# An RWKV layer with its decay totals moved to their own buffer and its hand-written order of steps rewritten on four engines

## The chip, the core and the metric

The kernel runs on one core of one Trainium2 chip, in one launch. The metric is the device time of that launch in microseconds: the median of the runs. All data are float32. Five kinds of engine work at once, each through its own list of instructions in the order in which they are written: TensorE (PE in the rows), VectorE (DVE), ScalarE (ACT), GpSimd (POOL) and SyncE (SP), whose queue starts the DMAs. They meet only at semaphores, so where an instruction waits, everything behind it on its engine waits too.

## What is computed

One RWKV layer over 8 batches of 256 tokens with 512 channels (32 heads of 16). Cut to what matters:

```python
xn  = ln(x) ;  sx = token_shift(xn)
xxx = tanh((xn + sx*maa_x) @ maa_w1) ; xxx = xxx @ maa_w2          # five small mixes
x5  = xn + sx*(maa_stack + xxx)                                    # five mixed inputs
w   = exp(-exp(time_decay + tanh(x5[1] @ decay_w1) @ decay_w2))
r, k, v, g = x5[3] @ Wr.T, x5[0] @ Wk.T, x5[2] @ Wv.T, silu(x5[4] @ Wg.T)
def step(s, rkvw):
    a = k[:, None] * v[None, :]
    return a + w[:, None]*s, r @ (u*a + s)                         # 256 steps in time, state 16x16 a head
att = groupnorm(scan(step)) * gn_w + gn_b
x   = x + (att*g) @ Wo.T
xn2 = ln(x) ; sx2 = token_shift(xn2)
kk  = relu((xn2 + sx2*ffn_maa_k) @ ffn_Wk.T)**2
x   = x + sigmoid((xn2 + sx2*ffn_maa_r) @ ffn_Wr.T) * (kk @ ffn_Wv.T)
```

## The kernel before, in words

A batch passes through four parts, and each part is cut into named steps. `n_` steps are the statistics and the norm of the raw input. `f_` steps (front) make the five mixed inputs and the projections k, v, r: `f_xin`, `f_lora0/1`, `f_m20` to `f_m24` (small matmuls of the mixes; `f_pair1`, `f_pair3` in the first batch), `f_mix0` to `f_mix4`, `f_dec1/2` (the decay), `f_k0` to `f_k3`, `f_v..`, `f_r..`. `b_` steps (back) are g (`b_g0` to `b_g3`), the recurrence inside blocks (`b_prod` on GpSimd, `b_score` on TensorE, `b_mul` and `b_red` on VectorE, `b_add` on GpSimd), the doubling of the decays over blocks of 1, 2, 4 and 8 tokens (`b_step1/2/4/8` on VectorE), the chunk states (`b_vtok`, `b_ktok`, `b_kv0/1`, `b_scan`, `b_exp`, `b_acc`, `b_apply0` to `3`), group norm, the output projection `b_wo` and the second layer norm. `c_` steps (tail) are the feed-forward part: `c_fk`, `c_fr0/1`, `c_fv0/1`, `c_mul`, `c_out`.

The work is pipelined over batches. `walk` (line 302) makes each engine's list: one round holds the tail of batch b-2, the back of batch b-1, the front of batch b and the norm of batch b+1. The rounds in order are `first` (front of batch 0), `second` (front of 1, back of 0), five times `main` (four of them in a hardware loop of two passes), `end`, `last`, and the feed-forward tail of batch 7. Which step follows which in a round is written out by hand for each engine and kind of round in the dictionary `ORDER` (lines 50 to 124).

The dictionary is the same for issue on every engine, but what a step waits for stands in the step. Those that matter here:

- `f_centre` (VectorE, lines 1436 to 1448) takes the head means out of the value weights. It waits for the DMA that loads `wv` (line 351, the first of the large loads).
- `f_xin` (lines 1185 to 1208) makes the input of the small mixes, channel tile by channel tile. In the first batch it waits for ScalarE's normed input. `f_lora1` on TensorE (line 605) waits for each tile of it.
- `b_step1` (line 1263) multiplies the decays into k and r once `b_prod0` has read them. The products of decays ("totals", lines 265 to 268 and 1258 to 1261) are kept in the tile `ktok`, which also holds the second norm's output (`cen`, `xhat2`). Line 1270 waits, before the first total is written, until TensorE has transposed that output.
- `b_norm2` on VectorE (line 1524) waits for ScalarE's copies of those same transposes.
- `b_exp` (line 1392, and line 1065 on ScalarE) spreads the scanned states over heads for `b_apply0` to `3` on TensorE, which take them in the order VectorE, ScalarE, VectorE, ScalarE. `f_mix1` to `4` run on GpSimd at about the same time.
- SyncE: `stage(b)` loads the raw input of batch b once four scores of batch b-2 are done. `turn(b)` swaps two halves of a small tile, `thB` to `thR`, once `f_lora0/1` of batch b are through their tanh.

## Time and profile before

| | us |
|---|---|
| median of 3 runs | 771.14 |
| lowest and highest run | 769.87, 771.64 |
| span of the profiled execution (first to last instruction) | 768.0 |
| first round (0 to 52.4) | 52.4 |
| second round (52.4 to 137.9) | 85.5 |
| five main rounds and the end round, by the start of `c_fk` | 90.4, 90.3, 88.2, 87.0, 88.3, 87.3 |
| last round and feed-forward tail | 98.5 |

The profile lists the span of the profiled execution and not its time as the runs measure it; the median lies 3.1 us above the span, for what is around the instructions. Rounds are told apart by the first instruction of `c_fk` (line 856), at 137.92, 228.27, 318.59, 406.82, 493.80, 582.12 and 669.46 us.

In a row of the timeline, the first number is the start in us from the span's start, the second the time from start to end, `xN` the number of instructions merged, and the bracket the idle time of the engine before them with what ended it. "issue" there is a wait for nothing that the profile shows.

### The profile page before, as it was taken

The numbers are of one execution on the slowest core, as the hardware profiler recorded it, in microseconds if no ns is written. First come the engines' busy times: TensorE is split into PE (matmuls) and PEld (weight loads), VectorE is DVE, ScalarE is ACT, GpSimd is POOL, SyncE is SP. The second block draws the span as 40 slices with busy tenths as digits, with TensorE's granted clock in tenths as the row PEclk, the third lists the DMA queues.
The fourth block names the chain that finished last, engine by engine and source line by source line (L and its number), as shares of the span: only waits on it lengthen the run. The fifth ranks groups of instructions, "written<-read, shape, count | busy, mean of one in ns | idle before, by whom it ended". The sixth has DMA issues, their size and how long they took to land.

```text
span 768.0 us, 17247 instructions
## 1 busy us (share of the span) xinstructions
PE 691.9 (90%) x7260; PEld 480.3 (63%) x7260; DVE 509.0 (66%) x771; ACT 326.8 (43%) x639; POOL 388.9 (51%) x223
## 2 busy tenths in 40 slices
PE   5895699998999999998999989998899989998577
PEld 4772477657775676756766577746767557755343
DVE  5739744696575865578565967578566858589641
ACT  2240653327441475325733276325733176405411
POOL 1148056565456654575555654565655656364100
PEclk9998989999999989999999999999999999999779
DMA  7900000002000110002000020002000020000000
GB/s 208 393 2 28 9 3 0 1 2 91 2 1 1 34 57 3 3 1 90 3 0 1 2 90 2 1 1 76 17 2 1 1 63 3 27 2 1 30 0 27
DMA packets 13130, 24.57 MB, mean 32 GB/s; under 512 B 3840, under 2 KB 5632, under 8 KB 12032
## 3 DMA queue, kind: packets, MB, share of 16 engines
q1 hardware_dynamic: 13056, 23.47, 8.9%
q8 instruction: 60, 0.98, 0.5%
q14 instruction: 14, 0.11, 0.0%
HBM read 18.35 MB, written 4.19 MB: 29 GB/s over the span
## 4 chain that ended last, share of the span: by engine, by line
PE 79%; ACT 8%; DVE 7%; issue 4%; POOL 1%; DMA 1%; POOLq 0%; SPq 0%; DVEq 0%; ACTq 0%
PE FB L578 26%; PE BAB L838 8%; PE FA L856 7%; PE FB L586 7%; PE FA L879 7%; PE BAB L751 4%; PE FA L656 4%; ACT wide L1017 2%; PE FB L621 2%; PE BAB L781 2%; ACT half L1072 2%; PE BAB L815 2%; PE BAB L569 2%; PE BAB L795 1%; PE FA L569 1%
## 5 line engine op out<-in xcount | busy, mean ns | idle before, releaser
L455 POOL TENSOR_TENSOR mixes<-mixes 128x1024 f32<-128x1024 f32 x30 | 78.7, 2623 | 133.9 <-ACT mixes L991 133.9
L493 POOL TENSOR_TENSOR pp<-rT,kT 128x2048 f32<-128x2048 f32 (+1 forms) x32 | 108.9, 3405 | 54.9 <-DVE rT L1256 51.4
L457 POOL TENSOR_TENSOR mixes<-mixes,xnT 128x1024 f32<-128x1024 f32 x30 | 74.5, 2483 | 2.4
L1351 DVE TENSOR_REDUCE half<-half 128x256 f32<-128x2048 f32 (+2 forms) x32 | 64.5, 2016 | 0.4
L578 PE MATMUL FB<-mixes,wg_s 128*128 128x256 f32 x256 | 62.5, 394 | 0.0
L578 PE MATMUL FB<-mixes,wv_s 128*128 128x256 f32 x256 | 62.3, 395 | 0.1
L578 PEld LDWEIGHTS FB<-mixes,wg_s 128*128 128x128 f32 x256 | 48.0, 194 | 22.5 <-issue 15.1
L856 PE MATMUL FA<-wide,fk_s 128*128 128x256 f32 x256 | 58.3, 387 | 2.2 <-DVE wide L1515 2.2
L578 PE MATMUL FB<-mixes,wk_s 128*128 128x256 f32 x256 | 59.7, 391 | 0.1
L1335 DVE TENSOR_TENSOR half<-BAB,vp 128x2048 f32<-128x2048 f32 x24 | 55.0, 2291 | 6.6 <-PE BAB L751 5.2
L586 PE MATMUL FB<-fr_s,wide 128*128 128x512 f32 x128 | 58.4, 599 | 0.0
L578 PE MATMUL FB<-mixes,wr_s 128*128 128x256 f32 x256 | 58.0, 380 | 0.0
L991 ACT ACTIVATE mixes<-FA,cols_s 128x256 f32<-128x256 f32 x116 | 45.4, 478 | 28.8 <-PE FA L656 28.0
L879 PE MATMUL FA<-fv_s,wide 128*128 128x512 f32 x128 | 57.7, 593 | 0.0
L856 PEld LDWEIGHTS FA<-wide,fk_s 128*128 128x128 f32 x256 | 49.7, 195 | 9.8 <-issue 2.9
L578 PEld LDWEIGHTS FB<-mixes,wv_s 128*128 128x128 f32 x256 | 48.3, 195 | 11.3 <-issue 4.7
L578 PEld LDWEIGHTS FB<-mixes,wk_s 128*128 128x128 f32 x256 | 49.1, 195 | 9.0 <-issue 2.3
L578 PEld LDWEIGHTS FB<-mixes,wr_s 128*128 128x128 f32 x256 | 48.0, 190 | 8.2 <-issue 2.4
L751 PE MATMUL BAB<-pp,hm_s 32*32 32x512 f32 (+2 forms) x1280 | 42.4, 558 | 10.9 <-POOL pp L493 9.6
L509 POOL TENSOR_TENSOR acc<-acc,half 128x512 f32<-128x512 f32 x32 | 41.0, 1281 | 18.7 <-DVE half L1351 16.5
L1115 ACT ACTIVATE wide<-FB 128x512 f32<-128x512 f32 x16 | 9.5, 597 | 95.3 <-PE FB L586 95.3
L838 PE MATMUL BAB<-wo_s,wide 128*128 128x512 f32 x112 | 49.2, 593 | 0.0
(159 smaller groups left out, 1313.5 us busy)
## 6 DMA issues: line engine op xcount, KB each, us to landing
pp<-x SPq DMA_DIRECT2D x8, 512.0 KB, 4.3
xt<-x SPq DMA_DIRECT2D x8, 512.0 KB, 3.7
out<-wide SPq DMA_DIRECT2D x7, 512.0 KB, 2.9
half<-wv SPq DMA_DIRECT2D x1, 1024.0 KB, 4.7
wk_s<-wk SPq DMA_DIRECT2D x1, 1024.0 KB, 7.1
wr_s<-wr SPq DMA_DIRECT2D x1, 1024.0 KB, 8.2
wg_s<-wg SPq DMA_DIRECT2D x1, 1024.0 KB, 10.2
wo_s<-wo SPq DMA_DIRECT2D x1, 1024.0 KB, 13.6
```

What stands on the lines that cost most here:

```text
L455: nc.gpsimd.tensor_tensor(slot, slot, sx, ALU.mult).then_inc(s_["mixm_ready"], 1)
L457: nc.gpsimd.tensor_tensor(slot, slot, xnT[:, :, 1:L + 1], ALU.add).then_inc(s_["mix_ready"], 1)
L493: ins = nc.gpsimd.tensor_tensor(pp[:, i % 2, 0:size].rearrange("p (n i j) -> p n i j", i=m, j=m), spread(r.unsqueeze(3), 3, m), spread(k.u ...
L578: ins = nc.tensor.matmul(dst[:, c * L:(c + 1) * L], weight[:, q, c * P:(c + 1) * P], src[:, q, :], start=(q == 0), stop=(q == C - 1))
L586: ins = nc.tensor.matmul(dst[:, t * E:(t + 1) * E], src[:, q, t * P:(t + 1) * P], weight[:, q, :], start=(q == 0), stop=(q == C - 1))
L751: ins = nc.tensor.matmul(groups[32 * c:32 * c + 32, g, 0:w], hm_s[rows, rows], pp[rows, i % 2, c * w:c * w + w], start=True, stop=True)
L838: ins = nc.tensor.matmul(BA[:, t * E:(t + 1) * E], (yb_end if last(b) else yb)[:, q, t * P:(t + 1) * P], big["wo"][:, q, :], start=(q == 0 ...
L856: ins = nc.tensor.matmul(FA[:, c * L:(c + 1) * L], big["fk"][:, q, c * P:(c + 1) * P], xk[:, q, :], start=(q == 0 and c % 2 == 0), stop=(q ...
L879: ins = nc.tensor.matmul(FA[:, t * E:(t + 1) * E], kk[:, q, t * P:(t + 1) * P], big["fv"][:, q, :], start=(q == 0), stop=(q == C - 1))
L991: ins = nc.scalar.activation(xmix[:, j % 3, c, :], mixed_in(b, j)[:, c * L:(c + 1) * L], ACT.Identity, bias=col(MAA_STACK + MIXES[j])(c))
L1335: nc.vector.tensor_tensor(product.rearrange("p (n i j) -> p n i j", i=m, j=m), BAB[:, :].rearrange("p (n i j) -> p n i j", i=m, j=m), spre ...
L1351: nc.vector.tensor_reduce(to, src, AX.X, ALU.add).then_inc(s_["qs_ready"], 1)
```

## The change

Three edits:

1. The totals of the decays get their own tile `totals_s` (4 KB in a partition), and `b_step1` no longer waits for `xhat2T_ready`.
2. SyncE does `turn(1)` ahead of `stage(2)`.
3. The lists of `ORDER` are rewritten. `last` is unchanged but for `c_out1` ahead of `c_out0` on GpSimd; `end` has few changes; `first`, `second` and `main` have many.

```diff
     tensor=dict(
         first="""
-            f_norm warm6 f_lora1 f_lora0 f_pair1 f_m20 f_k0 f_k1 f_k2 f_k3 f_dec1 f_pair3 f_dec2 f_v0 f_v1 f_v2
-            f_v3 f_r0 f_r1 f_r2 f_r3""".split(),
+            f_norm warm6 f_lora1 f_pair1 f_lora0 f_m20 f_k0 f_k1 f_k2 f_v0 f_dec1 f_v1 f_pair3 f_k3 f_dec2
+            f_v2 f_v3 f_r0 f_r1 f_r2 f_r3""".split(),
         second="""
-            b_g0 b_score0 f_norm b_g1 b_score1 b_score2 b_g2 b_score3 b_score4 b_g3 b_vtok f_lora0 b_ktok b_kv0
-            b_kv1 f_m20 f_lora1 f_dec1 f_m21 f_m22 b_acc b_apply0 b_apply1 f_dec2 b_apply2 f_m23 b_apply3 f_k0
-            f_k1 f_k2 f_v0 f_v1 b_gn0 b_gn1 f_k3 b_wo0 b_wo1 f_m24 f_v2 f_v3 b_norm20 f_r0 f_r1 b_norm21 f_r2
-            f_r3""".split(),
+            b_g0 b_g2 b_score0 b_g1 f_norm b_score1 b_g3 b_score2 b_score3 b_score4 f_lora0 f_lora1 b_vtok
+            f_m20 b_ktok f_m21 b_kv0 f_dec1 b_kv1 f_dec2 f_m22 f_m23 b_acc f_k2 b_apply0 b_apply1 f_k0 f_k1
+            b_apply2 b_apply3 f_k3 f_v0 f_v2 b_gn0 b_gn1 f_v1 b_wo0 b_wo1 f_m24 f_r0 f_r1 f_v3 b_norm20
+            b_norm21 f_r2 f_r3""".split(),
         main="""
-            c_fk b_score0 c_fr0 c_fv0 b_score1 b_g0 b_score2 f_norm c_fr1 b_score3 b_g1 b_g2 b_score4 b_g3 c_fv1
-            b_ktok f_lora0 f_lora1 b_vtok f_m20 f_m21 b_kv0 f_dec1 b_kv1 f_dec2 b_acc f_m22 f_k0 f_k1 f_k2 f_k3
-            b_apply0 b_apply1 b_apply2 b_apply3 f_v0 f_v1 f_m23 f_v2 b_gn0 b_gn1 f_m24 f_v3 b_wo0 b_wo1 f_r0
-            f_r1 b_norm20 b_norm21 f_r2 f_r3""".split(),
+            c_fk c_fr0 b_score0 b_g0 b_score1 c_fv0 b_score2 c_fr1 f_norm b_score3 b_g1 b_g2 b_score4 b_g3
+            c_fv1 f_lora0 b_ktok f_lora1 b_vtok f_m20 f_m21 b_kv0 f_dec1 b_kv1 f_dec2 b_acc f_m22 f_k0 f_k2
+            f_k1 b_apply0 b_apply1 f_k3 f_m23 b_apply2 b_apply3 f_v0 f_v1 f_v2 f_v3 b_gn0 b_gn1 f_r0 f_m24
+            b_wo0 b_wo1 f_r1 f_r2 b_norm20 b_norm21 f_r3""".split(),
...
     vector=dict(
         first="""
-            f_xin f_centre f_mix1 f_mix2 f_mix0 n_stats n_norm f_centre0""".split(),
+            f_centre f_xin f_centre0 f_mix1 f_mix2 n_stats f_mix0 n_norm""".split(),
         second="""
-            b_prodx b_step1 b_mul0 b_step2 b_mul1 b_red1 b_step4 b_gate0 b_mul2 b_red2 b_mul3 b_red3 b_mul4
-            b_step8 b_gate1 f_xin b_red4 f_mix0 b_kv b_scan b_exp b_var0 b_var1 b_root b_nrm0 b_nrm1 n_stats
+            b_prodx b_step1 b_mul0 b_step2 b_mul1 b_step4 b_red1 b_mul2 b_gate0 b_red2 b_mul3 b_gate1 f_xin
+            b_red3 b_mul4 b_red4 b_step8 f_mix0 b_kv n_stats b_scan b_exp b_var0 b_var1 b_root b_nrm0 b_nrm1
             b_gn b_wo0 b_wo1 b_xhat20 b_xhat21 b_norm2 n_norm b_xr""".split(),
         main="""
-            b_step1 b_mul0 b_step2 c_mul0 b_mul1 b_step4 b_red1 b_mul2 b_red2 b_mul3 b_gate0 b_red3 b_mul4
-            b_step8 f_xin b_gate1 c_mul1 b_red4 f_mix0 n_stats b_kv b_scan b_exp b_var0 b_var1 b_root b_nrm0
-            b_nrm1 b_gn b_wo0 b_wo1 b_xhat20 b_xhat21 n_norm b_norm2 b_xr""".split(),
+            b_step1 b_step2 b_mul0 b_mul1 b_step4 b_red1 c_mul0 b_mul2 b_red2 b_mul3 b_red3 b_mul4 b_step8
+            b_gate0 f_xin c_mul1 b_gate1 b_red4 f_mix0 n_stats b_kv b_scan b_exp b_var0 b_var1 b_root b_nrm0
+            b_nrm1 b_gn b_wo0 b_wo1 b_xhat20 b_xhat21 b_norm2 b_xr n_norm""".split(),
...
     gpsimd=dict(
         first="""
-            n_stats f_mix3 f_sx f_mix4""".split(),
+            f_mix3 f_sx f_mix4 n_stats""".split(),
         second="""
-            b_prod0 b_prod1 b_prod2 b_prod3 b_add1 b_prod4 b_add2 f_sx b_s0 b_add3 b_add4 f_mix1 f_mix2 f_mix3
-            b_wo0 b_wo1 f_mix4 n_stats""".split(),
+            b_prod1 b_s0 b_add1 b_prod2 f_sx b_prod3 b_prod4 b_add2 b_add3 f_mix1 b_add4 f_mix2 f_mix3
+            n_stats b_wo0 b_wo1 f_mix4 b_prod0""".split(),
...
     scalar=dict(
         first="""
-            f_norm f_lora0 f_lora1 f_k0 f_k1 f_dec1 f_mix3 f_mix4 f_v0 f_dec2 f_v1 f_r0 f_r1""".split(),
+            f_norm f_lora1 f_lora0 f_k0 f_dec1 f_v0 f_mix3 f_k1 f_dec2 f_mix4 f_v1 f_r0 f_r1""".split(),
         second="""
-            f_norm b_g0 b_rcopy b_g1 b_vtok b_ktok b_decays f_lora0 b_kv0 b_kv1 f_lora1 f_dec1 f_mix1 b_exp
-            f_mix2 f_dec2 b_sq0 b_sq1 f_k0 b_gn f_mix3 f_k1 f_mix4 f_v0 f_v1 b_norm2 f_r0 f_r1""".split(),
+            b_g0 f_norm b_g1 f_lora0 f_lora1 b_vtok b_ktok f_mix1 b_kv0 f_dec1 b_decays b_kv1 f_mix2 f_dec2
+            b_rcopy b_exp b_sq0 b_sq1 f_k0 f_k1 b_gn f_mix3 f_v0 f_mix4 f_v1 f_r0 b_norm2 f_r1""".split(),
         main="""
-            c_fk0 c_fk1 c_fr0 c_fr1 f_norm b_rcopy b_g0 b_decays b_g1 b_ktok f_lora0 f_lora1 b_vtok f_mix1 b_kv0
-            f_dec1 b_kv1 f_dec2 f_mix2 f_k0 b_exp b_sq0 b_sq1 f_k1 f_mix3 b_gn f_v0 f_v1 f_mix4 b_norm2 f_r0
-            f_r1""".split(),
+            c_fk0 c_fk1 c_fr0 f_norm c_fr1 b_g0 b_rcopy b_g1 f_lora0 b_ktok b_decays f_lora1 b_vtok f_mix1
+            b_kv0 f_dec1 b_kv1 f_dec2 f_mix2 b_exp f_k0 f_mix3 b_sq0 b_sq1 f_k1 f_v0 b_gn f_mix4 f_v1 f_r0
+            b_norm2 f_r1""".split(),
...
+        totals_s = sb("totals_s", [P, C * L])
...
-            return ktok[:, :, :].rearrange("p t e -> p (t e)")[:, at:at + C * L // m]
+            return totals_s[:, at:at + C * L // m]
...
+            turn(1)
             stage(2)
-            turn(1)
...
                         dve.wait_ge(s_["w_ready"], b + 1)
-                        if not first(b):
-                            dve.wait_ge(s_["xhat2T_ready"], T * b)
```

In the `end` round, TensorE does `f_m23` ahead of `b_apply0` and `f_k2` (it stood behind them), VectorE `b_step8` ahead of `f_xin`, and GpSimd `b_add3` and `b_s0` ahead of `c_out1`.

## Rows read from the trace of the kernel before

**Rows 1.** The page: TensorE's busy time and the chain's shares by engine
```profile
PE 691.9 (90%) x7260; PEld 480.3 (63%) x7260; DVE 509.0 (66%) x771; ACT 326.8 (43%) x639; POOL 388.9 (51%) x223
PE 79%; ACT 8%; DVE 7%; issue 4%; POOL 1%; DMA 1%; POOLq 0%; SPq 0%; DVEq 0%; ACTq 0%
```

**Rows 2.** Busy time by stretch: first, second and first main round
```profile
core 0: us, PE busy (x) PEld busy (x) DVE busy (x) ACT busy (x) POOL busy (x), PEclk, DMA share, GB/s
0.00:52.40 52.40, 39.87 (x244) 33.21 (x244) 25.32 (x52) 15.34 (x35) 13.16 (x17) 0.97 0.62 221
52.40:137.90 85.50, 67.48 (x832) 47.99 (x833) 56.11 (x84) 36.45 (x71) 42.50 (x24) 0.90 0.03 9
137.90:228.20 90.30, 86.17 (x905) 60.15 (x904) 62.40 (x95) 41.23 (x81) 52.23 (x28) 0.96 0.06 21
```

**Rows 3.** Timeline of VectorE in the first round
```profile
13.73 0.48 DVE L1196 SCALAR_TENSOR_TENSOR mixes<-mixes,cols_s,xnT 128x256 f32<-128x256 f32 x1
...
15.25 2.29 DVE L1433 TENSOR_REDUCE gT<-half 128x128 f32<-128x2048 f32 x1 [1.04 <-DMA half<-wv]
...
17.84 2.50 DVE L1443 TENSOR_TENSOR wv_s<-half,gT 128x512 f32<-128x512 f32 x4
...
20.45 1.66 DVE L1222 SCALAR_TENSOR_TENSOR mixes<-FA,cols_s,mixes 128x256 f32<-128x256 f32 x4
```

**Rows 4.** Timeline of TensorE and ScalarE in the first round
```profile
15.33 1.95 PE L632 MATMUL BAB<-mixes,w_s 128*64 128x256 f32 x16
...
18.76 0.37 ACT L953 ACTIVATE thR<-BAB 128x256 f32<-128x256 f32 x1
...
23.54 8.83 PE L578 MATMUL FB<-mixes,wk_s 128*128 128x256 f32 x32
...
49.41 1.89 PE L578 MATMUL FB<-mixes,wg_s 128*128 128x256 f32 x8
```

**Rows 5.** Timeline: VectorE's first product of the second round, and the next `c_fk`
```profile
50.48 1.23 DVE L1301 TENSOR_TENSOR pp<-half,kT 128x1024 f32<-128x1024 f32 x1 [16.28 <-ACT half L1136]
...
137.92 7.07 PE L856 MATMUL FA<-wide,fk_s 128*128 128x256 f32 x32
```

**Rows 6.** Timeline of the second round: VectorE and TensorE
```profile
74.39 2.29 DVE L1335 TENSOR_TENSOR half<-BAB,vp 128x2048 f32<-128x2048 f32 x1 [0.71 <-PE BAB L751]
...
91.99 2.29 DVE L1390 TENSOR_TENSOR_SCAN kvs<-pp,kvs 128x1024 f32<-128x1024 f32 x1
...
94.32 3.71 DVE L1398 TENSOR_TENSOR wide<-kvs,cm_s 128x1024 f32<-128x1024 f32 x2
...
107.22 5.45 PE L578 MATMUL FB<-mixes,wk_s 128*128 128x256 f32 x24
```

**Rows 7.** Timeline around the applies: first main round, then the fourth
```profile
191.66 5.85 DVE L1398 TENSOR_TENSOR wide<-kvs,cm_s 128x1024 f32<-128x1024 f32 x2
...
201.17 0.42 PE L815 MATMUL BAB<-half,rsplit 64*32 64x64 f32 x23 [1.31 <-issue]
201.53 5.41 PE L578 MATMUL FB<-mixes,wv_s 128*128 128x256 f32 x16
...
459.35 2.35 POOL L455 TENSOR_TENSOR mixes<-mixes 128x1024 f32<-128x1024 f32 x1 [3.23 <-ACT mixes L991]
459.49 7.59 DVE L1398 TENSOR_TENSOR wide<-kvs,cm_s 128x1024 f32<-128x1024 f32 x2
...
467.23 0.85 PE L815 MATMUL BAB<-wide,rsplit 64*32 64x64 f32 x64 [1.73 <-DVE wide L1398]
```

**Rows 8.** Timeline early in main rounds: GpSimd's first product, VectorE's `f_xin`, TensorE's `f_m21`
```profile
139.22 4.28 POOL L482 TENSOR_TENSOR pp<-half,kT 128x1024 f32<-128x1024 f32 x1 [5.26 <-ACT half L1136]
...
171.32 1.67 DVE L1205 SCALAR_TENSOR_TENSOR mixes<-mixes,cols_s,xnT 128x256 f32<-128x256 f32 x4
...
179.95 0.47 PE L656 MATMUL FA<-thB,w_s 32*128 32x256 f32 x1 [1.84 <-DVE mixes L1222]
...
319.20 3.36 POOL L482 TENSOR_TENSOR pp<-half,kT 128x1024 f32<-128x1024 f32 x1 [6.12 <-ACT half L1136]
```

39 lines of the change are left out of this document (20 added, 19 removed).

## The prediction

> **What bounds the kernel now.** I read the page first: TensorE is busy 90% of the span, and the chain that ended last runs through it for 79% [rows 1]. The busy time by round shows where it is not the bound. In the first main round TensorE works 86.2 of 90.3 us; in the second round only 67.5 of 85.5, at a mean granted clock of 0.90 [rows 2]. So a main round can give back a few us, the second round more, and what delays TensorE's first large projection is paid in full. The timelines then tell what each stall is. The sum is made against the profiled span, 768.0 us; the median of the runs is 771.14, 3.14 above it, and I carry that over unchanged.
>
> **The buffer, the wait and SyncE's order.** Line 1270 holds VectorE until TensorE has transposed the second norm of the batch before. VectorE has already done `b_norm2` of that batch, which waits for ScalarE's copies of the same transposes, in the new lists too. The wait is always met, and taking it out is worth 0. The buffer moves no time by itself: who writes `ktok` next, ScalarE's `b_ktok`, still waits for the last decay step. `turn(1)` ahead of `stage(2)` delays the load of batch 2 until `f_lora1` of batch 1 is through; its reader on VectorE comes more than 10 us after that in the new list, so 0. What is left is the order.
>
> **First round: +7.9.** VectorE's new list begins with `f_centre`, then `f_xin`. `f_centre` cannot start before the value weights have landed: its row starts at 15.25, released by that DMA, and its last part ends at 17.84 + 2.50 = 20.34 [rows 3]. Before, `f_xin` ran ahead of it and ended at 13.73 + 0.48 = 14.21, and the centring lay hidden while TensorE made the small matmuls: the first mix followed at 20.45, 0.11 after it [rows 3]. Now the four tiles of `f_xin` come behind it: a tile is two operations of 0.43 and 0.48 that overlap a little, 0.86 apart, so four end at about 23.9. Then comes what was hidden: the last quarter of `f_lora1` (0.5), the mirrored matmuls (1.95), their tanh (0.37) [rows 4], `f_pair1` (1.1) and four hand-overs of 0.1: 28.2. That is 7.8 after 20.45. From there the order of mix and `f_k0` is the same (23.54 - 20.45 = 3.1 us, rows 3 and 4), and from 23.54 to g at 49.41 TensorE had no stall worth naming [rows 4], with the same set of matmuls in another order. Nothing in the round can take the delay up. `f_lora0` behind `f_pair1` and the norm of batch 1 behind GpSimd's `f_mix4` cost 0 to 1; I take 0.1, since both have about 0.7 us of slack ahead of VectorE's first product. Bounds: +6.8 (hand-overs shorter, warm clock) and +9.2.
>
> **Second round: -0.5.** Counted from VectorE's first product (50.48) to `c_fk` (137.92), it takes 87.44 now [rows 5]. In the new list `b_gate1` (0.7) and `f_xin` (1.67, rows 8) stand ahead of `b_mul4`, and `b_step4` waits for its product with `b_red1` (1.2) behind it instead of ahead; in return the wait of 0.71 [rows 6] goes. So the last score's product starts some 2.8 later than 74.39 - 50.48 = 23.9. The chain from there (values transposed, spread by ScalarE, chunk states, scan) keeps its length, but `n_stats` (1.7) now stands ahead of `b_scan`, and GpSimd's `f_mix2` runs beside it. The scan ended at 91.99 + 2.29, which is +43.8 [rows 6]; it now ends 2.8 + 1.7 + 0.6 later, at +48.9. The two spreads took 3.71 together with GpSimd idle [rows 6], and 5.85 and 7.59 with GpSimd's mixes beside them [rows 7]; one GpSimd step (2.2) comes first here, so the first spread ends at +53.0 where `b_apply0` can start. `f_k0` and `f_k1` stand behind `b_apply1` (3.6, and 1.8 more if TensorE comes out of the wait at its lower clock, which I take), then two applies (1.3) end at +61. Before, attention was done where the k projections began, at 107.22, which is +56.7 [rows 6]. But three of the four column tiles of k, 5.45 us [rows 6], are done by then, and the 30.7 us from there to `c_fk` were without a stall. They become 30.7 - 5.45, and 0.7 for group norm that is no longer covered: `c_fk` at +86.9, so -0.5. Bounds: -4.5 if the first spread isn't held up and the clock stays, +2 if the lower clock lasts over `b_vtok` and the chunk states too.
>
> The trace shows the two engines in each other's way in pairs: in the fourth main round GpSimd's mix starts at 459.35 and takes its usual 2.35, VectorE's spread begins 0.14 later and two take 7.59 [rows 7]. The Trainium skill (SBUF — State Buffer, section "SBUF: two separate sides") says that a VectorE operation with two SBUF inputs and a GpSimd operation that reads SBUF lock each other out for the whole instruction, whichever came first. The trace agrees (459.35 + 2.35, then 3.7 for two spreads with one more GpSimd step between them). By that rule the scan, which also has two SBUF inputs, is held as I have it; without it the round would come to -2.8.
>
> **Main rounds: -3.4 in five.** Two things go, one comes.
> Around the applies: before, four applies run in one piece and stall in every round, by 1.31 for "issue" and 0.35 for ScalarE in the first, or by 1.73 for VectorE in the fourth [rows 7]; I found 1.3 to 1.8 in each of the five. Now `f_k3` and `f_m23` (1.8 + 1.0) stand between the second and the third apply. The stalls behind them vanish where VectorE's first spread wins against GpSimd (four of five); where GpSimd wins, `b_apply0`, now 1.8 earlier, waits about 0.6. That is 1.66 + 1.6 + 1.35 + 1.1 + 1.8 = 7.5. In the first main round the stall is followed by 16 matmuls in 5.41 instead of 3.6 [rows 7]: 1.8 more, and the clock should stay. Together -9.3. Only `f_r3` now covers the second norm ahead of `c_fk`, where two tiles did: +0.1 each, +0.5.
> At the start of a round: `c_fr0` goes ahead of `b_score0`, `b_step2` ahead of `b_mul0`, `b_gate0` ahead of `f_xin`, `n_norm` behind `b_xr`. TensorE reaches `f_lora0` when `f_xin` (1.67, rows 8) is still at work (+0.4) and `f_lora1` when `b_gate1` is (+0.15); before, `b_ktok` covered the one and `c_mul1` came after the gate. GpSimd's first product takes 3.36, or 4.28 when VectorE is at work on `b_xr` [rows 8], which it now always is; with the late one, `b_score1` finds VectorE's `b_mul0` unfinished (another +0.8). The wait of 1.84 ahead of `f_m21` [rows 8] stays: its cover is the same. So 0.6 to 1.6 a round; I take 1.1, +5.5 in five. Sum: -9.3 + 0.5 + 5.5 = -3.3, and -0.1 for SyncE's and ScalarE's small moves. Bounds: -9.5 (the start costs nothing) and +4 (one more stall of 1.5 in each round).
>
> **End and last: -0.1.** `f_m23` ahead of `b_apply0` fills a stall of 1.0, but `f_v0` behind them waits for the same GpSimd mix as before. `c_out1` ahead of `c_out0` changes the order of two operations that follow each other.
>
> **Sum:** 768.0 + 7.9 - 0.5 - 3.4 - 0.1 = 771.9, and with 3.14 around the span 775.0 us.
>
> **The rivals.**
> (a) The rounds give back more than the start loses. If the early part of the round costs nothing, since TensorE's own work still covers it, main gives 9.4, and the second round 2.8 to 4.5: 7.9 - 2.8 - 9.4 - 0.1 = -4.4, 766.7 us. For it: four of five rounds have a stall that the new order fills exactly. Against: VectorE is busy without a gap up to `f_xin`. It decides from 4 us gained in main beyond my sum. This is the rival on the other side. Chance 0.27.
> (b) Both about cancel, 769.6 to 772.7: half of that gain. Chance 0.15.
> (c) The clock. The row behind the stall of 1.31 ran at about two thirds of its speed [rows 7], and the second round's mean was 0.90 [rows 2]. If each of the new short waits at the start of a main round lets the clock fall, at 1.8 a time [rows 7], five rounds cost 9 more and I come to about 783. The page TensorE: Matmul & The Clock Gate of the Trainium skill (section "HAM oscillation — how this bites in real kernels") warns that idle gaps between bursts throttle the array again each time; the rows bear that out for one round in five. Chance 0.10.
> (d) The change doesn't do what it says: the buffer frees nothing, as above. This is in every case, not a case of its own.
> My own case, 771 to 779 with 775.0 in it, has 0.48. Slower is (c) and my case, 0.58.
> The least difference that a measurement of this kernel can tell is 0.2%, 1.5 us. The range reaches down to (a) and up to (c): 766.5 to 781.5.
>
> **What the profile after would show.** Right: `f_centre` starts at 15.25 and `f_xin` ends near 24; `f_k0` starts near 31.4 and VectorE's first product of the second round near 58.4; `c_fk` of the first main round near 145.3; no "issue" stall in the applies; waits of TensorE for `f_xin` and `b_gate1` at `f_lora0/1`; main rounds of about 88 us. Wrong would be a first product before 56 (then the start was covered by something I missed), main rounds under 86.5 (rival a), or over 90 with a granted clock below 0.96 (rival c).

## The result, and the profile after

The changed kernel took 795.48 us in the median (793.32 to 798.05), beside 770.80 for the kernel before: a ratio of 1.0315, interval 1.0272 to 1.0358. It is slower, as forecast, but by 24.7 us and not by 4. The profiled span is 791.5 us; the rest of this part splits its 23.5 us over 768.0. The other 1.2 us of the 24.7 are not in it: the profiled execution was the fastest of the changed kernel's four.

The page of the changed kernel: the span, the busy times, then the chain by engine.

```profile
span 791.5 us, 17240 instructions
PE 698.4 (88%) x7260; PEld 476.8 (60%) x7260; DVE 533.1 (67%) x771; ACT 326.4 (41%) x639; POOL 388.1 (49%) x223
...
PE 63%; DVE 23%; ACT 5%; issue 5%; POOL 2%; SPq 1%; DMA 1%; DVEq 0%; POOLq 0%; ACTq 0%
```

Against [rows 1], VectorE is busy 24 us longer with as many instructions as before (771), and its share of the chain rises from 7% to 23%, while TensorE's falls from 79% to 63%. The same operations of VectorE last longer, and TensorE waits for them. Where the time came in, by the start of `c_fk` in each round:

| stretch | before | after | change | forecast |
|---|---|---|---|---|
| up to VectorE's first product | 50.48 | 57.73 | +7.25 | +7.9 |
| from there to the first `c_fk` | 87.44 | 88.08 | +0.6 | -0.5 |
| five main rounds | 444.2 | 457.5 | +13.3 | -3.4 |
| - of it `c_fk` to the first `b_kv0` | 217.0 | 228.9 | +12.0 | +5.5 |
| - of it `b_kv0` to the first `f_k` | 40.3 | 41.5 | +1.2 | 0 |
| - of it `f_k` to the next `c_fk` | 187.0 | 187.1 | +0.1 | -8.8 |
| `end` round | 87.34 | 89.42 | +2.1 | -0.1 |
| last round and tail | 98.5 | 98.8 | +0.3 | 0 |

Busy time by stretch for the same three stretches as [rows 2] (first, second and first main round):

```profile
core 0: us, PE busy (x) PEld busy (x) DVE busy (x) ACT busy (x) POOL busy (x), PEclk, DMA share, GB/s
0.00:57.70 57.70, 38.70 (x241) 31.29 (x242) 23.29 (x49) 14.97 (x34) 13.15 (x17) 0.91 0.56 201
57.70:145.40 87.70, 68.25 (x835) 47.25 (x835) 64.52 (x82) 36.81 (x73) 44.03 (x24) 0.86 0.03 9
145.40:237.30 91.90, 87.17 (x907) 59.54 (x905) 64.31 (x93) 41.38 (x82) 50.85 (x28) 0.96 0.06 20
```

VectorE has 64.5 us of work in the second round where it had 56.1, with 82 instructions where it had 84. The granted clock of the first main round is 0.96 in both.

What TensorE waited for, in the changed kernel (total us, times, longest):

```profile
PE BAB L571 <- DVE ktok L1479: 12.2, 7, 5.8
...
PE FB L623 <- DVE mixes L1198: 9.0, 1, 9.0
...
PE BAB L753 <- DVE half L1320: 7.1, 5, 1.9
PE BAB L817 <- issue: 6.8, 5, 1.8
```

And the same view of the kernel before:

```profile
PE BAB L815 <- issue: 9.1, 8, 1.8
...
PE BAB L569 <- DVE ktok L1479: 5.8, 1, 5.8
```

Three waits are new. The single one of 9.0 is the first round's, for `f_xin` (line 1198). Five of up to 1.9 stand ahead of the second score (L753, for VectorE's `b_mul0` at line 1320), one a main round. And the group norm's product (L571, for line 1479) is now waited for in each main round, 1.1 to 1.2 us; before, the only such wait was the one of 5.8 in the last round, which is still there. The "issue" wait of the applies shrank from 9.1 to 6.8 over the whole kernel; in the five main rounds all waits inside the applies together fell from 8.1 to 0.8. The forecast had the wait for `f_xin` and the end of the stalls in the applies, the wait for `b_mul0` at 0.8 in some rounds, and nothing for the group norm.

### The profile page after: what moved, and what is told of

Its sections match the earlier page's. It is cut to its first block, busy times and chain, and to the rows that moved or that the text cites. A ratio compares the mean times of both kernels' runs of the same rounds, so it can differ in the third digit from the quotient of the medians.

```text
span 791.5 us, 17240 instructions
## 1 busy us (share of the span) xinstructions
PE 698.4 (88%) x7260; PEld 476.8 (60%) x7260; DVE 533.1 (67%) x771; ACT 326.4 (41%) x639; POOL 388.1 (49%) x223
## 4 chain that ended last, share of the span: by engine, by line
PE 63%; DVE 23%; ACT 5%; issue 5%; POOL 2%; SPq 1%; DMA 1%; DVEq 0%; POOLq 0%; ACTq 0%
PE FB L580 19%; PE FA L881 7%; PE BAB L840 7%; PE FB L588 5%; PE FA L658 4%; DVE wide L1515 4%; PE BAB L753 3%; PE BAB L817 3%; PE FA L858 2%; PE BAB L783 2%; PE BAB L571 2%; PE FB L623 2%; POOL pp L495 2%; ACT wide L1019 1%; DVE half L1351 1%
## 5 line engine op out<-in xcount | busy, mean ns | idle before, releaser
L1351 DVE TENSOR_REDUCE half<-half 128x256 f32<-128x2048 f32 (+2 forms) x32 | 64.5, 2015 | 0.5
L858 PE MATMUL FA<-wide,fk_s 128*128 128x256 f32 x256 | 59.9, 394 | 3.6 <-DVE wide L1515 3.5
L580 PE MATMUL FB<-mixes,wg_s 128*128 128x256 f32 x256 | 60.9, 387 | 0.0
L753 PE MATMUL BAB<-pp,hm_s 32*32 32x512 f32 (+2 forms) x1280 | 43.3, 569 | 19.6 <-POOL pp L495 9.1
L881 PE MATMUL FA<-fv_s,wide 128*128 128x512 f32 x128 | 59.9, 612 | 0.0
L580 PE MATMUL FB<-mixes,wv_s 128*128 128x256 f32 x256 | 58.5, 383 | 0.0
L658 PE MATMUL FA<-thB,w_s 32*128 32x256 f32 x120 | 37.3, 433 | 12.7 <-DVE mixes L1224 10.3
## 6 DMA issues: line engine op xcount, KB each, us to landing
wg_s<-wg SPq DMA_DIRECT2D x1, 1024.0 KB, 10.5
```

Of the source, the lines that this page charges most:

```text
L580: ins = nc.tensor.matmul(dst[:, c * L:(c + 1) * L], weight[:, q, c * P:(c + 1) * P], src[:, q, :], start=(q == 0), stop=(q == C - 1))
L658: return nc.tensor.matmul(bank[:, c * L:(c + 1) * L], w2_s[rows, c * P:c * P + P], (thB, thR)[half_of][rows, :], start=True, stop=True)
L753: ins = nc.tensor.matmul(groups[32 * c:32 * c + 32, g, 0:w], hm_s[rows, rows], pp[rows, i % 2, c * w:c * w + w], start=True, stop=True)
L858: ins = nc.tensor.matmul(FA[:, c * L:(c + 1) * L], big["fk"][:, q, c * P:(c + 1) * P], xk[:, q, :], start=(q == 0 and c % 2 == 0), stop=(q ...
L881: ins = nc.tensor.matmul(FA[:, t * E:(t + 1) * E], kk[:, q, t * P:(t + 1) * P], big["fv"][:, q, :], start=(q == 0), stop=(q == C - 1))
L1351: nc.vector.tensor_reduce(to, src, AX.X, ALU.add).then_inc(s_["qs_ready"], 1)
```

## The experiments

Eighteen kernels, each against the kernel before on the same chip. Those called "before + ..." have the lists of before with the part named, and all of them have the new buffer, the dropped wait and SyncE's new order too. "Main" is the sum of the five main rounds of the profiled execution. In kernels whose main lists are those of before it reads 444.2, 444.0, 440.8, 443.1 and 447.6, so one reading carries some 3 us either way.

| run | what it is | median | ratio, 95% interval | main |
|---|---|---|---|---|
| before | | 769.8 to 775.5 by job | 1 | 444.2 |
| after | all of the change | 795.5 | 1.0315, 1.0272 to 1.0358 | 457.5 |
| e1_buffer_only | before's lists, new buffer, no wait, SyncE's turn | 770.3 | 1.0018, 0.9992 to 1.0044 | 444.0 |
| e2_first_only | before + new `first` | 775.3 | 1.0093, 1.0042 to 1.0144 | 440.8 |
| e9_new_second | before + new `second` | 772.6 | 0.9995, 0.9964 to 1.0025 | 443.1 |
| e10_new_main | before + new `main` | 784.4 | 1.0126, 1.0058 to 1.0193 | 461.2 |
| e11_new_end | before + new `end` | 774.9 | 1.0017, 0.9981 to 1.0053 | 447.6 |
| e3_xin_first | after, `f_xin` ahead of `f_centre` | 792.8 | 1.0305, 1.0271 to 1.0338 | 455.5 |
| e4_mix3_later | after, ScalarE's `f_mix3` later | 810.1 | 1.0533, 1.0477 to 1.0588 | 472.2 |
| e5_mix3_after_root | after, `f_m23` and `f_mix3` as before | 800.4 | 1.0416, 1.0313 to 1.0520 | 461.1 |
| e6_old_start | after, old start of `main` | 785.9 | 1.0202, 1.0115 to 1.0289 | 448.2 |
| e7_old_tail_too | e5 + old tail of `main` | 779.4 | 1.0127, 1.0037 to 1.0217 | 441.5 |
| e13_n_norm_first | after, `n_norm` ahead of `b_norm2` | 789.9 | 1.0238, 1.0176 to 1.0299 | 451.9 |
| e16_before_n_norm_last | before, `n_norm` behind `b_xr` | 772.9 | 0.9991, 0.9952 to 1.0029 | 445.2 |
| e14_before_new_applies | before + new applies | 794.4 | 1.0261, 1.0201 to 1.0322 | 469.2 |
| e17_new_applies_short_mix | e14, short mix on GpSimd | 769.3 | 0.9963, 0.9932 to 0.9994 | 449.9 |
| e8_before_split_applies | before + split applies | 768.2 | 0.9951, 0.9915 to 0.9987 | 443.8 |
| e15_split_again | the same, on another chip | 768.4 | 0.9926, 0.9893 to 0.9958 | 439.2 |
| e18_split_short_mix | e15, short mix | 769.6 | 0.9958, 0.9924 to 0.9992 | 443.5 |
| e12_before_e7_main | before + the `main` of e7 (new start, split applies, ScalarE's `b_exp` ahead of `f_k0`, old tail) | 771.0 | 0.9977, 0.9947 to 1.0007 | 442.1 |

### One part alone

The buffer, the dropped wait and SyncE's order, with `ORDER` of before put into the changed kernel:

> The kernel before with the totals in their own tile, without the wait for the second norm's transposes, and with turn(1) ahead of stage(2); all orders as before. My theory: the wait was always met and the buffer frees nobody, so the span stays at 768 (+-1.5) and c_fk of the first main round starts at 137.9. Rival (the tile itself or SyncE's order costs, by another place in SBUF or a later load): several us more, seen in the second round.

Measured 770.3, ratio 1.0018: nothing, as rival (d) had it. The whole difference is the order.

The new `first` alone:

> The kernel before with the new first lists on all engines (and the buffer), the other rounds as before. Theory: the start's loss is a shift that nothing behind it takes up, so VectorE's first product of the second round starts at 57.7 instead of 50.5 and the span is 768 + 7.3 = 775. Rival (later rounds take a part of it up, since they wait for loads or for slower engines anyway): under 771.

Measured 775.3. VectorE's first product is at 58.75, 8.3 later; the second round then takes 84.96 instead of 87.44 in this profile; the eleven other kernels with the old lists of `second` read 86.2 to 89.0, so the 2.5 given back are mostly scatter.

The new `second`, `main` and `end`, each alone:

> The kernel before with the new lists of the round `second` alone, on all four engines. Theory (the parts add up; the second round of the changed kernel took 88.1 to 90.0 us where before has 87.4, though it began on a clock already raised): the second round costs 1 to 3 us, 773. Rival (the second round is slow only behind the new first round): within 1 us, 771.

> The kernel before with the new lists of the five main rounds alone, on all four engines. Theory (the parts add up): the main rounds lose the 13 us that they lost in the changed kernel, and the round `end` that follows one more at its start, so 784 to 786. Rival (much of the main rounds' loss is a lower clock that the longer first round left behind): 776 to 780.

> The kernel before with the new lists of the round `end` alone (f_m23 ahead of b_apply0 and f_k2 on TensorE, small changes on the others). Theory (f_m23 waits for its input and holds the first apply: the wait there grows from 1.0 to 1.8 us and no later wait goes): +1 us, 772. Rival (the loss in `end` was in its start, from the main tail): 771.

`second` shows no loss in the medians (the rival), but its interval leaves room for 2 us, and the profiles lean that way: in the eight kernels with the new lists the round reads 88.1 to 91.7 from VectorE's first product (89.5 in this one), in the twelve with the old ones 85.0 to 89.0. `main` alone costs 12.0 us in the medians, 17.0 in the profiled rounds, which are those of its slowest execution: it needs no first round to be slow. `end` has a round of 89.43 where before has 87.34, with the old main rounds ahead of it, so that loss is in its own list; in the medians its +2.6 is inside the interval. By ratio the four parts add to 0.93 + 1.26 + 0.17 - 0.05 = 2.3%, and the change as a whole costs 3.15%; with `main` taken from its profiled rounds (17.0 of 768, 2.2%) the sum would be 3.3%. Whether the parts simply add is therefore open by some 6 us.

Why `end` loses I read from three engines' timelines around its first apply; no run puts back one step of `end` alone. The kernel with the new `end` alone:

```profile
638.73 2.36 POOL L452 TENSOR_TENSOR mixes<-mixes 128x1024 f32<-128x1024 f32 x1 [3.15 <-ACT mixes L988]
638.95 7.53 DVE L1393 TENSOR_TENSOR wide<-kvs,cm_s 128x1024 f32<-128x1024 f32 x2
...
642.88 0.85 PE L812 MATMUL BAB<-wide,rsplit 64*32 64x64 f32 x64 [1.84 <-issue]
643.65 3.10 PE L575 MATMUL FB<-mixes,wk_s 128*128 128x256 f32 x8
```

and before:

```profile
635.80 5.81 DVE L1398 TENSOR_TENSOR wide<-kvs,cm_s 128x1024 f32<-128x1024 f32 x2
636.09 3.82 POOL L455 TENSOR_TENSOR mixes<-mixes 128x1024 f32<-128x1024 f32 x1 [3.66 <-ACT mixes L991]
...
637.82 0.85 PE L815 MATMUL BAB<-wide,rsplit 64*32 64x64 f32 x64 [1.00 <-issue]
638.60 2.00 PE L578 MATMUL FB<-mixes,wk_s 128*128 128x256 f32 x8
```

Before, VectorE's spread begins 0.29 ahead of GpSimd's mix, which has to wait (3.82 instead of 2.36). In the new list ScalarE copies for `b_rcopy` behind `f_mix2` instead of ahead of it, the mix comes 0.22 ahead of the spread, and now it is the spread that waits. `f_m23` ahead of the apply hides 1.2 of that, 1.84 stay, and the eight matmuls behind take 3.10 instead of 2.00, at a granted clock of 0.63 where before it is 1.00. In the changed kernel the mix is 0.23 ahead and the wait is 1.84 as well, but those matmuls take 1.99: there 1.2 of the 2.1 come in here, and 0.9 at the start of the round, behind the new tail of the last main round (0.1 with `n_norm` put back, in the run below).

### The first round

```diff
         first="""
-            f_centre f_xin f_centre0 f_mix1 f_mix2 n_stats f_mix0 n_norm""".split(),
+            f_xin f_centre f_centre0 f_mix1 f_mix2 n_stats f_mix0 n_norm""".split(),
```

> The changed kernel with one pair swapped: VectorE does f_xin ahead of f_centre in the first round, as before. Theory: this pair alone is the start's loss; VectorE's first product of the second round starts at 50.5 (+-0.5) instead of 57.7 and the span falls by 7.2, to 784. Rival (other moves of the first round cost too, such as the norm of batch 1 behind GpSimd's last mix): it falls by less than 5.

Measured 792.8 (ratio 1.0305 beside 1.0315), far from the 784 expected. VectorE in this run:

```profile
22.97 0.69 DVE L1428 TENSOR_REDUCE gT<-s_s 128x32 f32<-128x512 f32 x1 [2.37 <-DMA s_s<-s]
...
24.30 1.65 DVE L1219 SCALAR_TENSOR_TENSOR mixes<-FA,cols_s,mixes 128x256 f32<-128x256 f32 x4
```

`f_centre0`, which the change also moved ahead of the mixes, waits 2.37 for the load of the initial state, and holds the first mix until 24.30 (20.45 before, 28.99 after). In the changed kernel that wait was hidden behind the first one. TensorE waits 6.55 for that mix and comes out of it at the lower clock (0.50 in the rows from 26 to 30 us), so its first 24 matmuls of k take 7.17 where the changed kernel has 5.42. VectorE's first product comes at 55.5, so the swap gives back 2.2 us of the start and not the whole 7.25. The second round of this execution takes 91.65, more than any other with these lists, and by the ratios (1.0305, 1.0315) no gain is told from zero.

### The start of a main round

With the old lists of the start on all four engines (TensorE below; VectorE up to `b_red4`, GpSimd up to `b_add4`, ScalarE up to `b_vtok`):

```diff
-            c_fk c_fr0 b_score0 b_g0 b_score1 c_fv0 b_score2 c_fr1 f_norm b_score3 ... f_lora0 b_ktok f_lora1 b_vtok
+            c_fk b_score0 c_fr0 c_fv0 b_score1 b_g0 b_score2 f_norm c_fr1 b_score3 ... b_ktok f_lora0 f_lora1 b_vtok
```

> The changed kernel with the lists of the kernel before for the start of the five main rounds on all four engines (TensorE up to b_vtok, VectorE up to b_red4, GpSimd up to b_add4, ScalarE up to b_vtok); middle and end of the round stay new. Theory (the start's order costs): from c_fk to kv0 the round loses again most of the 12.0 us that it gained: 9 us less, 786. Rival (the start is late because VectorE's b_xr and n_norm, which stand in the round's new tail, now run beside GpSimd's first product, and b_step1 is late for that alone): b_step1's first operation still comes 7 to 8 us after c_fk and no more than 3 us come back: 792 to 795.

With only `n_norm` put back, and the same edit made the other way in the kernel before:

```diff
-            b_nrm1 b_gn b_wo0 b_wo1 b_xhat20 b_xhat21 b_norm2 b_xr n_norm""".split(),
+            b_nrm1 b_gn b_wo0 b_wo1 b_xhat20 b_xhat21 n_norm b_norm2 b_xr""".split(),
```

> The changed kernel with VectorE's n_norm ahead of b_norm2 in the main rounds, and nothing else undone. Theory (n_norm at the end is what pushes b_xr beside GpSimd's b_prod0): b_xr's last six operations take 2.5 us instead of 5.8, b_step1 starts at 5 to 6 us of c_fk, the waits ahead of b_score1 shrink by a half, and the start gives back 1 us a round: 790. Rival (the tail on TensorE, with f_r2 ahead of b_norm20, does it): b_xr still ends after GpSimd's product has begun, within 1.5 us of the changed kernel.

> The kernel before with VectorE's n_norm behind b_xr in the main rounds, and nothing else. Theory (n_norm at the end pushes b_xr beside GpSimd's first product, and b_step1 behind it): b_xr slows to 5.8 us or n_norm to 3.0 and b_step1 comes 1 to 2.5 us later; TensorE's old start has b_score0 and c_fr0 to cover that, so 0 to 3 us more, 771 to 774. Rival (n_norm must be early because the next stage waits for it): 5 us more or above.

And with the whole old tail (TensorE below, VectorE's `n_norm`, and ScalarE's `b_gn f_v0 f_v1 f_mix4 b_norm2 f_r0 f_r1`), on top of the old places of `f_m23` and `f_mix3`:

```diff
-            ... f_v2 f_v3 b_gn0 b_gn1 f_r0 f_m24 b_wo0 b_wo1 f_r1 f_r2 b_norm20 b_norm21 f_r3
+            ... f_v2 b_gn0 b_gn1 f_m24 f_v3 b_wo0 b_wo1 f_r0 f_r1 b_norm20 b_norm21 f_r2 f_r3
```

> As the run with f_mix3 after the root, and with the tail of the main rounds of the kernel before as well (TensorE behind f_v0, ScalarE behind f_mix3, VectorE's n_norm ahead of b_norm2); the start and the split of the applies stay new. Theory (the tail puts b_xr beside GpSimd's product): b_xr's six operations take 2.5 us again instead of 5.8, b_step1 starts at about 6.1 of c_fk, and against the run with f_mix3 alone another 5 us come back: 784. Rival (the start's own order costs it): within 1.5 us of that run.

From `c_fk` to `b_kv0`, summed over five rounds:

| before | after | old start | `n_norm` first | old tail too |
|---|---|---|---|---|
| 217.0 | 228.9 | 216.5 | 222.6 | 220.5 |

The second score's wait for `b_mul0` is what TensorE loses: 1.0, 1.8, 0.7, 1.8 and 1.9 us in the five rounds of the changed kernel, 7.1 in all (the waits above), and none before. The rows show VectorE at the start of the third main round (`c_fk` at 330.29) and TensorE's wait there, then TensorE in the fifth (`c_fk` at 511.12), where the clock is at 0.57 behind the wait and `c_fv0` takes 5.40 instead of 3.60:

```profile
330.00 5.79 DVE L1515 SCALAR_TENSOR_TENSOR wide<-wide,cols_s 128x256 f32<-128x256 f32 x6
335.71 0.99 DVE L1169 TENSOR_SCALAR kvs<-pp,mv,rs 128x512 f32<-128x512 f32 x2
...
341.21 0.78 DVE L1253 TENSOR_TENSOR kT<-kT,totals_s 128x512 f32<-128x512 f32 x1 [2.22 <-POOL pp L495]
...
342.51 1.21 DVE L1317 TENSOR_TENSOR acc<-BAB,vp 128x1024 f32<-128x1024 f32 x1
...
344.47 0.73 PE L753 MATMUL BAB<-pp,hm_s 32*32 32x256 f32 x32 [0.70 <-DVE half L1320]
...
526.40 0.73 PE L753 MATMUL BAB<-pp,hm_s 32*32 32x256 f32 x32 [1.92 <-DVE half L1320]
527.06 5.40 PE L881 MATMUL FA<-fv_s,wide 128*128 128x512 f32 x8
```

Before, the six operations of `b_xr` took 2.46 there and ended ahead of `b_step1`; here they take 5.79, as one of them waits for GpSimd's `b_prod0`. Then `n_norm` (0.99) runs, and `b_step2` (with a wait of 2.22 for GpSimd) stands ahead of `b_mul0`, for which the second score waits.

- Putting `n_norm` back alone gives 6.3 of the 12.0 back. My expectation had the size (1 us a round) but not the way: `b_xr` still takes 5.79 in that run. What goes is `n_norm`'s own 0.99 on the path to `b_step1` in the last four rounds: the waits of the second score fall to 1.0, 0.9, 0.3, 0.9 and 1.0, and the clock no longer falls in the fifth (1.8). In the first main round nothing changes there (`n_norm` takes 3.03 in both runs), since what stands ahead of it is the tail of `second`.
- So it is not `n_norm` that brings `b_xr` beside GpSimd's product. Its last six operations begin 0.6 ahead of `c_fk` before, and 0.7 to 0.9 behind it in the changed kernel and in this run alike (in three of the last four rounds). With the old tail they begin 0.6 ahead again and take 2.46. That leaves the tail of TensorE or of ScalarE; on TensorE one tile of r (`f_r3`) stands behind the second norm where there were two. Neither was put back alone.
- The old start gives back all of it (216.5), although `b_xr` is as slow there (5.79). In the old list the second score stands at 15 us of `c_fk`, behind `c_fr0` and `c_fv0`, and VectorE's `b_mul0` is ready by then.
- In the kernel before, putting `n_norm` behind `b_xr` stretches `n_norm` to 4.22 and costs nothing (0.9991). So the late `n_norm` is harmless under the old start and costs 6.3 under the new one.

The cause of the +12.0 is therefore the pair: VectorE late by its tail, and a TensorE list in which only `b_g0` (2 us) lies between the first score and the second, while VectorE has to make both `b_step2` and `b_mul0` in that time. The old start undoes all of it; the old tail 8.4, so the new start costs 3.6 by itself and the new tail nothing by itself. Which of the moves in the start does it (`c_fr0`, `b_step2` or the others) I read from the rows; they were only put back together.

### Around the applies

First attempts inside the changed kernel. Only ScalarE's `f_mix3` behind `f_k1`:

```diff
-            ... f_mix2 b_exp f_k0 f_mix3 b_sq0 b_sq1 f_k1 f_v0 b_gn f_mix4 ...
+            ... f_mix2 b_exp f_k0 b_sq0 b_sq1 f_k1 f_mix3 f_v0 b_gn f_mix4 ...
```

> The changed kernel with ScalarE's f_mix3 of the main rounds behind b_sq0, b_sq1 and f_k1, as before. GpSimd then begins its mix 3 later. Theory: the stall of TensorE at the group norm (1.2 us in each main round) comes from VectorE's root, whose second operation took 2.2 us instead of 0.2 beside GpSimd's mix 3; with the mix later that operation takes 0.2, the stall goes, and five main rounds give 1.2 to 1.5 each, 6 to 7 in all: span 785. Rival (the stall is TensorE's own, its four v tiles no longer cover the root): the stall stays and the span stays at 791.5 (+-1.5).

TensorE's `f_m23` behind `f_v1` as well:

```diff
-            f_k1 b_apply0 b_apply1 f_k3 f_m23 b_apply2 b_apply3 f_v0 f_v1 f_v2 f_v3 b_gn0 b_gn1 f_r0 ...
+            f_k1 b_apply0 b_apply1 f_k3 b_apply2 b_apply3 f_v0 f_v1 f_m23 f_v2 f_v3 b_gn0 b_gn1 f_r0 ...
```

> The changed kernel with one thing of the applies put back in the five main rounds: the product f_m23 stands behind f_v1 on TensorE and the copy f_mix3 behind f_k1 on ScalarE, as in the kernel before, so that GpSimd's part of f_mix3 starts after VectorE's square root of the group norm. Theory (the root is held by GpSimd's mix): the root's operation takes 0.2 us instead of 2.2 in all five rounds, TensorE's wait ahead of the group norm's product (1.1 to 1.2 us a round) is gone, so 5 to 6 us less: about 789. Rival (the wait for the norm is only where slack of another chain is used up, TensorE will be held at the group norm's product all the same or one step later): 793 to 796 with short roots.

The first came out slower than the changed kernel (810.1), the second no faster (800.4, above its rival's 793 to 796 too). The root in the first of them, beside GpSimd:

```profile
216.24 2.39 DVE L1421 SCALAR_TENSOR_TENSOR grs<-gsum,grs 128x64 f32<-128x64 f32 x1
218.66 2.21 DVE L1418 TENSOR_TENSOR gsum<-grs 128x64 f32<-128x64 f32 x1
...
216.20 2.35 POOL L452 TENSOR_TENSOR mixes<-mixes 128x1024 f32<-128x1024 f32 x1 [5.54 <-ACT mixes L988]
218.63 2.16 POOL L454 TENSOR_TENSOR mixes<-mixes,xnT 128x1024 f32<-128x1024 f32 x1
```

The mix moved into the middle of the root, and two of its operations of 0.22 last 2.39 and 2.21, each as long, within 0.05, as a GpSimd operation beside it. TensorE then waits 2.9 ahead of the group norm's product in every main round, and in four of the five its clock falls behind that wait. In the second the root is short in every round, but the new tail has `f_r0` right behind the group norm, and `f_r0` waits for that mix ("issue", five times, up to 1.9): the stall moved by one step, as the rival had it.

Then the parts in the kernel before. The new middle of the round, without the new tail (on ScalarE `f_k0 b_exp b_sq0 b_sq1 f_k1 f_mix3` becomes `b_exp f_k0 f_mix3 b_sq0 b_sq1 f_k1`):

```diff
-            ... f_k0 f_k1 f_k2 f_k3 b_apply0 b_apply1 b_apply2 b_apply3 f_v0 f_v1 f_m23 f_v2 b_gn0 b_gn1 ...
+            ... f_k0 f_k2 f_k1 b_apply0 b_apply1 f_k3 f_m23 b_apply2 b_apply3 f_v0 f_v1 f_v2 b_gn0 b_gn1 ...
```

> The kernel before with the new middle of the main rounds alone on TensorE and ScalarE (f_k0 f_k2 f_k1 b_apply0 b_apply1 f_k3 f_m23 b_apply2 b_apply3, and f_mix3 ahead of b_sq0). Theory (the stalls of the applies go, 7.5 us, but VectorE's root waits 2 us for GpSimd's mix, and the group norm's product waits 1.2 us a round): the rounds win at most 2 us in all, 769 to 772, with the root's operation at 2.2 us. Rival (the prediction's term): 8 to 9 us less, 763.

It takes 794.4: both expectations missed, by over 20 us. The second main round of this run, VectorE, GpSimd and TensorE in the timeline, then the busy time by stretch:

```profile
296.43 0.66 DVE L1412 TENSOR_SCALAR gve<-gvar 128x64 f32<-128x64 f32 x1
297.12 2.21 DVE L1413 TENSOR_SCALAR gsum<-gve 128x64 int32<-128x64 int32 x1
...
294.68 2.36 POOL L452 TENSOR_TENSOR mixes<-mixes 128x1024 f32<-128x1024 f32 x1 [1.65 <-ACT mixes L988]
297.11 2.17 POOL L454 TENSOR_TENSOR mixes<-mixes,xnT 128x1024 f32<-128x1024 f32 x1
...
302.75 1.81 PE L566 MATMUL BAB<-ident_s,ktok 128*128 128x128 f32 x8 [2.95 <-DVE ktok L1474]
306.50 3.60 PE L575 MATMUL FB<-mixes,wv_s 128*128 128x256 f32 x8
```

```profile
core 0: us, PE busy (x) PEld busy (x) DVE busy (x) ACT busy (x) POOL busy (x), PEclk, DMA share, GB/s
299.00:302.80 3.80, 0.85 (x5) 0.42 (x3) 3.42 (x14) 0.00 (x0) 0.28 (x1) 1.00 0.00 0
302.80:305.00 2.20, 2.20 (x10) 1.76 (x12) 0.72 (x3) 0.83 (x2) 0.00 (x0) 0.54 0.00 0
305.00:307.00 2.00, 2.00 (x9) 1.18 (x6) 1.50 (x4) 1.58 (x4) 0.00 (x0) 0.50 0.00 0
307.00:309.00 2.00, 2.00 (x6) 1.55 (x5) 0.00 (x0) 0.00 (x0) 0.00 (x0) 0.50 0.00 0
```

Both GpSimd operations fall on the start of the root: the first holds an operation for 0.46, the second one for 2.0. TensorE stands 2.95 ahead of the group norm's product, and behind that wait its granted clock falls to 0.54 and 0.50, the lower of its two levels (1.2 GHz), for some 7 us. Eight matmuls take 3.60 instead of 1.99. Each of the five rounds shows this (`b_gn0` to `b_wo0` 6.8 to 7.5 us instead of 3.9), and the five rounds together take 25.0 more: with the wait and the clock behind it, a held operation of 0.2 us goes with 5 us a round. The changed kernel has `f_v3` ahead of the group norm as well, waits only 1.22, and keeps its clock.

To see whether GpSimd is the cause or merely beside it, its `f_mix3` was made short, with all waits as they are; and as a control the same in the kernel whose mix stands behind the root. Both leave part of the fourth mixed input unfinished. The text on record calls it a quarter; by its rows it is an eighth (128 of 1024 columns).

```diff
                     slot = xmix[:, j % 3]
+                    part = slice(0, 32) if j == 3 else slice(0, L)
+                    slot = slot[:, :, part]
-                    nc.gpsimd.tensor_tensor(slot, slot, sx, ALU.mult).then_inc(s_["mixm_ready"], 1)
+                    nc.gpsimd.tensor_tensor(slot, slot, sx[:, :, part], ALU.mult).then_inc(s_["mixm_ready"], 1)
...
```

(The addition behind the product is cut to the same columns.)

> The run with the new applies alone, with one cost taken away: GpSimd's two operations of f_mix3 work on 32 of each 128 columns (a quarter), so the fourth mixed input is left unfinished in the other columns; everything else, order and waits, is the same. Theory (VectorE's root is held for as long as GpSimd's operation runs, and the clock falls for the wait that follows): the root's operation takes at most 0.8 us instead of 2.2, TensorE's wait ahead of the group norm's product falls from 3.0 to under 1 us, the clock stays up, and most of the 22 us come back: 768 to 775. Rival (the wait comes from f_m23 and f_mix3 elsewhere, not from GpSimd's operation): 785 or above.

> The kernel before with f_k3 between b_apply1 and b_apply2, and the same quarter of f_mix3 on GpSimd. As the mix stands behind the root here, theory expects nothing from its length: within 2 us of the run with the split alone, 766 to 770. If it comes out 5 us or more below, the short mix helps by another way and the run beside it proves less.

```profile
296.53 0.46 POOL L454 TENSOR_TENSOR mixes<-mixes 128x128 f32<-128x128 f32 x1 [1.66 <-ACT mixes L991]
...
298.52 0.20 DVE L1416 TENSOR_SCALAR gsum<-gve 128x64 int32<-128x64 int32 x1
...
302.13 1.32 PE L569 MATMUL BAB<-ident_s,ktok 128*128 128x128 f32 x8 [0.48 <-DVE ktok L1477]
```

769.3 instead of 794.4 (by ratio 0.9963 instead of 1.0261, 3.0%), and the control doesn't move (769.6 beside 768.4, ratio 0.9958 beside 0.9951 and 0.9926). The length of GpSimd's operation is the cause of the 20 to 25 us. The wait for the group norm is 0.48 here. (The profiled execution of this run was its longest, with a span of 776.9: in two rounds the applies wait and the clock falls, as in the last section.)

Last, the split alone, with `f_m23` and `f_mix3` left behind the root:

```diff
-            ... f_k0 f_k1 f_k2 f_k3 b_apply0 b_apply1 b_apply2 b_apply3 f_v0 f_v1 f_m23 ...
+            ... f_k0 f_k1 f_k2 b_apply0 b_apply1 f_k3 b_apply2 b_apply3 f_v0 f_v1 f_m23 ...
```

> The kernel before with one part of the change alone: in the five main rounds f_k3 stands between b_apply1 and b_apply2 on TensorE. Theory of the prediction (the stall in the third apply, 1.3 to 1.8 us a round, goes, as GpSimd's and ScalarE's part arrive under f_k3, and nothing else is in the way as f_mix3 stays behind f_v1): 5 to 7 us less, 764 to 766. Rival (the saved time is handed on to the group norm, where TensorE must wait for VectorE's chain of variances and root, which didn't move): the stall moves there, 769 to 771.

> The kernel before with the split of the applies alone (f_k3 between b_apply1 and b_apply2 in the main rounds), again, in five rounds on another chip. If its gain of 0.5% stands: ratio 0.993 to 0.998. If it was scatter: 0.998 to 1.002.

0.9951 and 0.9926 on two chips: 4 to 6 us, and faster than both kernels. The main rounds of the second take 439.2 instead of 444.2. TensorE's waits ahead of the applies ("issue" and ScalarE):

```profile
PE BAB L812 <- issue: 6.2, 7, 1.6
...
PE BAB L812 <- ACT half L1069: 3.1, 4, 0.8
```

The "issue" waits fall from 9.1 to 6.2; new are four short ones for ScalarE's first spread, as `b_apply1` comes 1.8 earlier. That is the prediction's term, in the right direction and at half to three quarters of the 7.5 put on the stalls.

And the new start with it (the `main` lists of the run with the old tail, all else as before):

> The kernel before with the main rounds of the run that had the old tail and the old places of f_m23 and f_mix3 (so the start and the split of the applies are new, the rest is old). Theory (its five rounds took 441.5 us where before has 444.2, and nothing else differs from before): 2 to 3 us less than before, 768 to 769. Rival (rounds of equal lists differ by as much between executions, and the new start costs 0.4 a round): within 1 us of before, 770 to 772.

The new start with the old tail and the split together: 0.9977, and its interval reaches 1. Its five starts read 44.5, 43.9, 44.0, 43.9 and 44.2 where before has 43.2 to 43.7, 3.6 more in all. From the first `f_k` to the next `c_fk` its five rounds take 180.3, and 180.6 in the run with the old tail, where before has 187.0 and the plain split 183.0 and 184.0: here ScalarE's `b_exp` stands ahead of `f_k0`, the waits of 0.8 are gone in three of five rounds, and with `f_mix3` left behind the root nothing takes the gain away. So the start takes back about half of what the applies give.

## Why the prediction was right or wrong

- **Buffer, wait, SyncE: 0.** Right (1.0018).
- **First round: +7.9.** Right: +7.25. `f_centre` started at 15.33 (forecast 15.25), `f_xin` ended at 23.82 (24), the first mix came at 28.99 (28.2), `f_k0` at 32.08 (31.4), the first product at 57.73 (58.4):

```profile
15.33 2.29 DVE L1433 TENSOR_REDUCE gT<-half 128x128 f32<-128x2048 f32 x1 [7.07 <-DMA half<-wv]
...
28.99 1.66 DVE L1224 SCALAR_TENSOR_TENSOR mixes<-FA,cols_s,mixes 128x256 f32<-128x256 f32 x4 [3.77 <-PE BAB L658]
...
32.08 5.42 PE L580 MATMUL FB<-mixes,wk_s 128*128 128x256 f32 x24
...
57.73 1.22 DVE L1301 TENSOR_TENSOR pp<-half,kT 128x1024 f32<-128x1024 f32 x1 [0.66 <-ACT half L1138]
```

  The text counted the handover at the load but not that `f_centre0` has a load of its own behind it, which makes the obvious repair worth only 2.2.
- **Second round: -0.5.** +0.6 measured, inside its bounds, and in part by luck: the scan ended 51.3 after VectorE's first product and not 48.9, but the two tiles of k between the applies took 3.7 at the full clock, where the text had put 5.4. Both together brought the applies to an end at 61.7 (61 forecast). The other kernels with these lists read up to 3.6 more.
- **Start of a main round: +5.5.** The mechanism was right and its size off: 2.4 a round, not 1.1. The step that failed is "0.6 to 1.6 a round" (its three items add to 1.35, so even the upper end had no term behind it). It put 0.8 on `b_score1`'s wait for `b_mul0`, in the rounds where `b_xr` is held, and 0.55 on waits at `f_lora0/1`. The second kind did not occur. The first was 1.4 on the mean (7.1 in five), for the text didn't ask what lies between the first score and the second: `b_g0` alone, 2 us, where before `c_fr0` and `c_fv0` gave 7.3. One of these waits cost 1.8 more by the clock, 1.1 came in behind `b_vtok`, and the rest (2 us) is 0.1 to 0.6 a round in hand-overs that the rows don't put down to a wait.
- **Around the applies: -9.3.** The gain itself came: in the changed kernel the stalls inside the applies are 7.3 less in five rounds, and the 1.7 that the lower clock cost in the first are gone. The step that failed is that this was taken as a gain to the end of the round, with nothing put for what moved along. The text moved `f_m23` and `f_mix3` ahead and did not move what they start: GpSimd's part of the mix, 4.5 us, which goes from behind the group norm's root to the top of it. There it makes a new wait ahead of the group norm's product, 6.0 in five rounds; 0.9 more come in up to `b_wo0`, and behind it about 2.4, where the text had put 0.5 for the second norm (both estimates, from the differences of the stretches). Together they use up the gain: +0.1 from `f_k` to `c_fk` and not -8.8. Without the new tail's extra tile of v as cover, as in the run with the new applies alone, the same move costs 5 us a round. The text had quoted the rule: the Trainium skill (SBUF — State Buffer, section "SBUF: two separate sides") lets a GpSimd operation hold a VectorE one for its whole length. The runs agree, 0.20 against 2.21 beside a mix of 2.17. As quoted it is for VectorE operations with two SBUF inputs; the operation held here has one, so the rows go beyond that sentence. I applied it to the spreads, which are long, and not to the operations of 0.2 us behind them. The kernel before had shown it too, in its `end` round, where a mix falls on the root; there other work covered it and TensorE did not wait:

```profile
646.01 2.18 POOL L457 TENSOR_TENSOR mixes<-mixes,xnT 128x1024 f32<-128x1024 f32 x1
...
646.02 2.22 DVE L1418 TENSOR_SCALAR gsum<-gve 128x64 int32<-128x64 int32 x1
```

- **`end`: -0.1.** +2.1 in its round. The step that failed is that a stall of 1.0 would be filled: it grew to 1.84. The text put nothing for ScalarE's list of `end`, where `b_rcopy` went behind `f_mix2`; by the rows that turned a lead of 0.29 for VectorE's spread into a lead of 0.22 for GpSimd's mix. 0.9 of the 2.1 come in at the round's start, from the main rounds' tail.
- **Rival (c), the clock.** It is not what the changed kernel lost by: its main rounds have a granted clock of 0.96 to 0.98, those of before 0.96 to 1.00, and of the new short waits at a round's start one in five was followed by the lower level (1.8). None of the three signs of being wrong fits: the rounds are over 90, but not with a clock below 0.96. But it is what makes the same fault cost 5 us a round in the run with the new applies alone.
- **The range** was said to reach "up to (c)", but (c) is 775.0 + 9 = 784 (about 783 in the text), and the range ended at 781.5. With every term at its upper bound the sum would be about 786, still 9 under the measured 795.5. The worst of the main rounds was taken as +4, one more stall of 1.5 a round. There were two new stalls in each of them, together 2.6 (1.4 and 1.2), and `end` and the clock came on top.

## What to carry to other kernels

When a step moves, follow what it starts on the other engines, and lay those operations beside everything that stands in their new place; a chain of a dozen short dependent VectorE operations is a bad place for a GpSimd operation, since one of 0.2 us that is held lasts until the GpSimd operation ends. Count cover by what lies between a product and its next reader on the bound engine, not by the length of the round. And an order that is good in one part can depend on another: here the late `n_norm` was free under the old start and cost 6.3 us under the new one, so try each part of a new order alone before its sum.

## What the runs showed of the hardware that I had not expected

- Single VectorE operations that take 0.20 to 0.23 us (128x64) elsewhere took 2.2 to 2.4 beside a GpSimd operation of 2.2 to 2.4. The held ones include a `TENSOR_SCALAR` with a single input tile, not only those with two; `n_norm`'s pair went from 1.00 to 3.03 and to 4.22.
- In the pairs read here the engine that starts first wins, by 0.2 to 0.3 us, and the loser pays 1.5 to 2 us: the spread of 638.95 behind the mix of 638.73 (7.53 instead of 5.81), and the mix of 636.09 behind the spread of 635.80 (3.82 instead of 2.36).
- A wait of 2.95 ahead of the group norm was followed by the lower clock in all five rounds of one kernel, one of 2.9 in four of five of another (`e4_mix3_later`), and one of 1.1 to 1.2 in none of the changed kernel's. In between it varies: 1.92 in one round of the changed kernel with the clock down to 0.57, 1.8 in two others without; and the stall of 1.31 in the applies of the kernel before [rows 7] has 0.50 behind it. The kernel with the new `main` alone has one round in which the applies wait 1.17 and then 2.06, and the clock falls:

```profile
384.00:386.00 2.00, 2.00 (x8) 1.35 (x6) 0.00 (x0) 0.00 (x0) 0.00 (x0) 0.64 0.04 8
386.00:388.00 2.00, 2.00 (x9) 1.18 (x8) 0.00 (x0) 0.00 (x0) 0.00 (x0) 0.50 0.00 0
```

  That round's stretch from the first apply to `f_v0` takes 10.5 us, and 5.9 to 7.0 in the four others. Which rounds fall is not settled by these runs.
